# Attention outputs brought to one layout by sixteen transfers a batch and divided there, in place of turns on TensorE, in a three-stage decoder layer on one Trainium2 core

## What is computed

```python
q = q.reshape(B, N, H, D).transpose(0, 2, 1, 3)          # H = 16 heads, D = 16 dims
scores = jnp.einsum('bhqd,bhkd->bhqk', q, k) / jnp.sqrt(jnp.asarray(D, q.dtype))
attn = jax.nn.softmax(scores, axis=-1)
out = jnp.einsum('bhqk,bhkd->bhqd', attn, v)
out = out.transpose(0, 2, 1, 3).reshape(B, N, C)
return out @ Wo.T + bo
```

## Time and profile before

| | us |
|---|---|
| median of three executions | 1017.08 |
| lowest and highest | 1014.64 and 1022.38 |
| the profiled execution | 1020.84 |
| its span, from the first to the last instruction | 1019.1 |

### The profile page before, as it was taken

How to read it: one execution, slowest core, us unless ns; L and a number is a source line. 1 busy time by engine, 2 the same in 40 slices (tenths; PEclk the granted TensorE clock), 3 DMA queues, 4 the chain that set the end, 5 groups by cost and what they waited for, 6 DMA issues and landing times. The chain is left out here.

```text
span 1019.1 us, 16854 instructions
## 1 busy us (share of the span) xinstructions
PE 863.1 (85%) x5964; PEld 663.5 (65%) x5964; DVE 597.7 (59%) x1441; ACT 405.0 (40%) x623; POOL 354.1 (35%) x290
## 2 busy tenths in 40 slices
PE   5998947789899888988989888887279999999993
PEld 4776725455666566655666556544279999999993
DVE  4889751545675777667676666643235555555542
ACT  4565611145444444445444454443043334233320
POOL 0333352222233434344342443223212442244422
PEclk9999967679998999999999998877579999999997
DMA  3117302444443445444344442400343222343100
GB/s 115 42 43 210 108 24 78 113 106 126 104 126 115 109 111 125 124 113 114 103 124 121 117 114 74 116 21 24 106 135 109 94 88 90 113 128 106 46 22 22
DMA packets 73432, 98.82 MB, mean 97 GB/s; under 512 B 10529, under 2 KB 60874, under 8 KB 73376
## 3 DMA queue, kind: packets, MB, share of 16 engines
q1 hardware_dynamic: 69920, 89.95, 32.0%
q0 software_dynamic: 3456, 8.13, 2.2%
HBM read 63.40 MB, written 35.73 MB: 97 GB/s over the span
## 5 line engine op out<-in xcount | busy, mean ns | idle before, releaser
L946 DVE TENSOR_REDUCE nmax<-ps_m 128x4 f32<-128x1024 f32 x128 | 156.6, 1224 | 174.6 <-PE ps_m L711 172.1
L903 ACT ACTIVATE pt<-ps_a 128x1024 f32<-128x1024 f32 x128 | 131.1, 1025 | 89.7 <-PE ps_a L721 88.3
L1216 ACT ACTIVATE hid<-ps_h 128x640 fp32r<-128x640 f32 x64 | 45.1, 705 | 151.3 <-PE ps_h L1156 151.3
L1156 PE MATMUL ps_h<-xt,w_hi 128*128 128x320 f32 x512 | 99.9, 318 | 1.0 <-DVE xt L1231 1.0
L1168 PE MATMUL ps_y<-w_hi,hid 128*128 128x256 f32 x640 | 85.3, 284 | 1.7 <-issue 1.7
L1265 DVE SCALAR_TENSOR_TENSOR hid<-ps_h,hid 128x640 fp32r<-128x640 f32 x64 | 52.7, 824 | 56.2 <-ACT hid L1216 55.7
L1156 PEld LDWEIGHTS ps_h<-xt,w_hi 128*128 128x128 f32 x512 | 80.0, 191 | 5.5 <-DVE hid L1265 3.9
L1168 PEld LDWEIGHTS ps_y<-w_hi,hid 128*128 128x128 f32 x640 | 80.1, 192 | 1.9 <-issue 1.9
L721 PE MATMUL ps_a<-qst,kst 49*128 49x256 f32 x512 | 67.8, 345 | 15.5 <-ACT pt L903 15.2
L721 PEld LDWEIGHTS ps_a<-qst,kst 49*128 49x128 f32 x512 | 40.8, 197 | 57.0 <-issue 31.8
L711 PE MATMUL ps_m<-kst,qst 48*128 48x256 f32 x512 | 66.9, 342 | 11.1 <-DVE nmax L946 5.9
(11 more groups left out here) (169 smaller groups left out, 1654.9 us busy)
## 6 DMA issues: line engine op xcount, KB each, us to landing
halves_dram<-half SPq DMA_DIRECT2D x64, 256.0 KB, 2.4
gated<-in_w SPq DMA_DIRECT2D x16, 1024.0 KB, 5.4
kst<-halves_dram SPq DMA_DIRECT2D x64, 128.0 KB, 3.1
qst<-halves_dram SPq DMA_DIRECT2D x64, 128.0 KB, 3.2
rows_dram<-blank SPq DMA_DIRECT2D x1, 5160.0 KB, 19.7
gated<-rows_dram SPq DMA_DIRECT2D x8, 645.0 KB, 4.2
x_raw<-in_x_t SPq DMA_DIRECT2D x8, 512.0 KB, 3.9
xres<-in_x SPq DMA_DIRECT2D x16, 256.0 KB, 3.6
```

The source lines that it names most:

```text
L903: nc.scalar.activation(pt[:, k % 4].rearrange("p s t q -> p (s t q)"), ps_a[:].rearrange("p s t q -> p (s t q)"), ACT.Exp).then_inc(s["exp ...
L946: nc.vector.tensor_reduce(nmax[:, q, :, :, h // 2].rearrange("p t s -> p s t"), ps_m[:], AX.X, ALU.max, negate=True).then_inc(s["max_done" ...
L1156: mm = pe.matmul(ps_h[:, f % 2, c2, 0:HC], w1[a][:, p, k, f * P:(f + 1) * P], xt[:, b, p, k, c2 * HC:(c2 + 1) * HC], start=(n == 0 and k = ...
L1216: nc.scalar.activation(hid[:, HI, f, :].rearrange("p (c n) -> p c n", c=2), ps_h[:, f % 2, :, 0:HC], ACT.Relu).then_inc(s["hid_hi"], 1)
```

## The change

The turns and the division by query are taken out: `sums_by_query`, lines 1028 and 1029, the turn back and the ScalarE copy. Instead `oraw` is sent on by transfers within SBUF (`part`): for each half of the heads eight, each 16 partitions of 512 elements (32 KB), which bring the dims of all heads to `odim` and their sums to `osum`, both with channels on partitions. VectorE then takes the reciprocal of the whole `osum` (128x512) and multiplies, in slot 9 of step `j+3`. `project_out` moves from slots 12 and 13 to 11 and 12, the residual and statistics from slot 14 to 13, their mean from 15 to 14. On SP `part` for the second half of the heads stands between the stores of keys and of queries, and for the first half behind the load of the context; both waits for landed stores now stand behind the stores of the queries. In `vals` two heads share one block of ones (48 columns for a pair instead of 64), so that in the second half of the heads the sums stand ahead of the dims; the ScalarE copy into `vals` writes the same elements in another order. The rows of `w_o` and `bv` are reordered on the host to fit.

```diff
-    vals = T("vals", [P, 2, KT, NH, VW], F32)
+    vals = T("vals", [P, 2, KT, NP, VP], F32)
...
-    rec = T("rec", [P, NH], F32)
-    onrm = T("onrm", [P, KT, D], F32)
+    odim = T("odim", [P, KD, S], F32)
+    osum = T("osum", [P, KD, S], F32)
...
+    o_in = [[s["lo_in0"], s["lo_in1"]], [s["hi_in0"], s["hi_in1"]]]
+    OIN = 2 * PV * 16
...
-                sp.wait_ge(stored, j * 32 + 32)
+
+            def part(j, p, side):
+
+                settled(sp)
+                sp.wait_ge(s["oraw_hi" if side else "oraw_lo"], j + 1)
+                need(sp, s["ont_out"], j)
+                for i in range(PV):
+                    rows = slice(NP * HD // 2 * side + HD * i, NP * HD // 2 * side + HD * (i + 1))
+                    for tile, odd in ((odim, side), (osum, 1 - side)):
+                        first = VW * i + HD * odd
+                        sp.dma_start(tile[rows, :, :], oraw[first:first + HD, 2 * side:2 * side + 2, :]
+                                     ).then_inc(o_in[side][p], 16)
...
                     store(n, p, 0, s["k_split"], s["k_stored"])
+                if on(n, 3):
+                    part(n - 3, 1 - p, 1)
+                if on(n, 0):
                     store(n, p, 1, s["q_split"], s["q_stored"])
+                    settled(sp)
+                    sp.wait_ge(s["k_stored"], n * 32 + 32)
+                    sp.wait_ge(s["q_stored"], n * 32 + 32)
                     stack(n, p, 0)
                 if on(n, 0) and on(n, -1):
                     load_ctx(n + 1, 1 - p)
+                if on(n, 2):
+                    part(n - 2, p, 0)
...
-                        mm = pe.matmul(ps_o[VW * i:VW * (i + 1), g, :], vals[:, p, t, h, :],
+                        odd = g // 2
+                        mm = pe.matmul(ps_o[VW * i:VW * (i + 1), g, :],
+                                       vals[:, p, t, g % 2 * PV + i, HD * odd:HD * odd + VW],
...
-                    if h in (7, 9) and on(n, 3):
-                        sums_by_query(n - 3, (h - 7) // 2)
-                    if h == 11 and on(n, 3):
-                        pe.wait_ge(s["on_done"], 2 * (n - 3) + 2)
-                        turn(ps_e, onrm, s["ont_mm"])
-                    if h in (12, 13) and on(n, 3):
-                        project_out(n - 3, h - 12)
+                    if h in (11, 12) and on(n, 3):
+                        project_out(n - 3, h - 11)
...
-                    if h == 12 and on(n, 3):
-                        act.wait_ge(s["ont_mm"], n - 2)
-                        nc.scalar.copy(ont[:].rearrange("p k t -> p (k t)"), ps_e[:]).then_inc(s["ont_out"], 1)
...
-                    if h in (8, 10) and on(n, 3):
-                        t = (h - 8) // 2
-                        dve.wait_ge(s["ot_mm"], 2 * j + t + 1)
...
-                        oc.done(nc.vector.reciprocal(rec[:], o4[:, :, HD]))
-                        nc.vector.tensor_tensor(onrm[:, t].rearrange("p (h d) -> p h d", d=HD), o4[:, :, 0:HD],
-                                                rec[:, :, None].to_broadcast([P, NH, HD]), ALU.mult
-                                                ).then_inc(s["on_done"], 1)
-                    if h == 14 and on(n, 3):
+                    if h == 9 and on(n, 3):
+                        dve.wait_ge(o_in[0][q], use(j, OIN, q))
+                        dve.wait_ge(o_in[1][q], use(j, OIN, q))
+                        need(dve, s["oproj_mm"], j)
+                        oc.done(nc.vector.reciprocal(osum[:], osum[:]))
+                        nc.vector.tensor_tensor(ont[:], odim[:], osum[:], ALU.mult).then_inc(s["ont_out"], 1)
+                    if h == 13 and on(n, 3):
                         dve.wait_ge(s["oproj_mm"], j + 1)
```

More of the change, by code:

```diff
@@ L391, in attend @@
     VW = 2 * HD
+    VP = 3 * HD
     AL, WL = 3, 5
@@ L739, in weigh @@
                 mm.then_inc(s["pv_mm"], 1)
-            def sums_by_query(j, t):
-                if t == 0:
-                    pe.wait_ge(s["oraw_hi"], j + 1)
-                    need(pe, s["place_done"], j)
-                else:
-                    pe.wait_ge(s["on_done"], 2 * j + 1)
-                for g in range(4):
-                    mm = pe.transpose(ps_e[:, g * P:(g + 1) * P], oraw[:, g, t * P:(t + 1) * P], eye[:])
-                mm.then_inc(s["ot_mm"], 1)
             def project_out(j, t):
@@ L753, in project_out @@
                     pe.wait_ge(s["ont_out"], j + 1)
+                    need(pe, s["place_done"], j)
                 for k in range(KD):
@@ L841, in split_hi, with sums_out @@
                 nc.scalar.copy(half[:, 0], kq[:]).then_inc(hi, 1)
-            def sums_out(j, half_of, done):
+            def sums_out(j, p, half_of, done):
                 act.wait_ge(s["pv_mm"], NG4 * j + NG4 // 2 * (half_of + 1))
-                need(act, s["ot_mm"], 2 * j)
+                if not isinstance(j, int) or j > 0:
+                    act.wait_ge(o_in[half_of][1 - p], use(j - 1, OIN, 1 - p))
                 two = slice(2 * half_of, 2 * half_of + 2)
@@ L940, in step @@
                 dc = Steps(dve, s["d_step"], 1, n)
-                oc = Steps(dve, s["o_step"], 3, j)
+                oc = Steps(dve, s["o_step"], 2, j)
                 rc = Steps(dve, s["r_step"], 4, i)
@@ L1038, in step @@
                         stats(st2, c["r2"], s["stats2"])
-                    if h == 15 and on(n, 3):
+                    if h == 14 and on(n, 3):
                         mean_var(oc, st2, mv2, s["stats2"], j)
@@ L1408, in by_dim, with by_side @@
         return np.moveaxis(v.reshape(v.shape[:-1] + (KD, P // HD // 2, 2, HD)), -3, -1).swapaxes(-2, -3).reshape(v.shape)
+    def by_side(v):
+        return v.reshape((2, KD, D // 4) + v.shape[1:]).swapaxes(0, 1).reshape(v.shape)
     mix, att, ffn = "L0_attn_", "L0_xattn_", "L0_ffn_"
@@ L1423, in laid_out @@
     }
-    for n in "vo":
-        arrays["w_" + n] = a(att + "W" + n).T
+    arrays["w_v"] = a(att + "Wv").T
+    arrays["w_o"] = by_side(a(att + "Wo").T)
     for n in "qk":
```

16 lines of the change are left out of this document (7 added, 9 removed).

## The result

| | before | after |
|---|---|---|
| median, us | 1017.21 (four executions, 1014.64 to 1022.38) | 1094.32 (four, 1093.73 to 1098.82) |
| ratio, with 95% interval | 1 | 1.0761 (1.0710 to 1.0812) |
| span of the profiled execution, us | 1019.1 | 1092.4 |
| mean granted clock | 0.909 | 0.865 |

The changed kernel is 7.6% slower, 77 us. The prediction said slower, but by 13 us, and its range ended at 1047.

What follows compares the result with a forecast made beforehand. TensorE, 90% busy and answered by VectorE, was taken as the bound. Steps +5.7, end of the stage +2 and clock +5 made +13 us on the median of 1017.08: 1030 us, range 1004 to 1047 (about 8 in 10).

Steps and rivals of the forecast that it cites:

- the two places: TensorE waits for `ont` at the projection (+0.45 us) and for `y` at line 674 (+0.4 us) in a full-clock step.
- The turns at full clock: Removing three groups of four turns on TensorE saves 0.7, 1.2 and 1.0 us, 2.9 us a step at most.
- The wait for `y`: TensorE waits about 1.5 us ahead of line 674, since residual and statistics stand ahead of `y` on VectorE.
- The end: Last step, from `oraw` copy to residual: +4.1 us; the two steps before give back 2 us, net +2 us.
- I let four steps of the 13 get an added half-clock stretch, each at 1.2 us: TensorE's longer waits bring extra time at half clock in four of 13 steps: +5 us in all.
- the multiplication has a row: 0.68 us: VectorE's added 128x512 multiplication takes 0.68 us, read from the earlier trace.
- the wait of 2 us: TensorE reaches the projection's first half at 381.0 us and waits 2 us for `ont`, there at 383.0.
- The short operations end near 378.45: In the full-clock step VectorE's short operations end at 378.45 us, before the transfers land at 379.0 and release the reciprocal.
- The second place: Line 674, needing `y`, starts 5.25 us behind line 711 where it was 4.85: +0.4 us a step.
- a period of 31 to 33 us: Sign in the changed profile: time between two executions of the once-a-step line, counterpart of line 951.
- all four cases: Rivals: reciprocal 0.7 us (993 us, 15%), 1.9 us (1006, 15%), 4.4 us (1045, 12%); late transfers (1045, 13%).
- the short-reciprocal case (993): Rival: VectorE's reciprocal takes 0.7 us, so `ont` is ready before TensorE: -1.8 us a step, 993 us; chance 15%.

Runs made afterwards that it cites:

- e4_no_divide: The changed kernel with the reciprocal and the multiplication left out, so the result lacks the division: 1029.67 us, ratio 1.0116.
- e9_no_divide_stats_late: The changed kernel without reciprocal and multiplication, and with the residual and its statistics back behind `y`: 992.07 us, ratio 0.9758.
- e12_residual_late: The changed kernel with POOL's two tensor additions for the residual issued behind its small powers: 1076.95 us, ratio 1.0528.
- late-projection kernels: The changed kernel with projection in slots 13 and 14, statistics in 15; division whole, in halves or in quarters: 1095.54, 1045.48, 1053.69 us.

## Why the prediction was wrong, by its steps

**Right.** The bound and the two places: TensorE waits for `ont` and for `y`, and the reciprocal takes 3.35 us where 3.3 was worked out from the earlier trace rows. The Trainium skill, "VectorE: DVE Perf Modes", section "Walkthrough: the 8-slice pipeline in each mode", read as 8 cycles for each element, would have given 4.4; the trace disagrees with that reading. The turns at full clock: "2.9 us a step at most", and 2.9 were measured (30.96 to 28.07). The wait for `y`: about 1.5 us, and 1.57 were measured; the 5.25 us from line 711 to line 674 were 5.24 in `e4_no_divide`. The end: from the end of the `oraw` copy to the start of the residual the last step needs 14.5 us where the earlier trace rows have 9.5, +5.0 against +4.1. On the queues there was luck: the issue was too low (0.42 us against 0.59), the landing too high (3.0 against 2.0), and the two errors nearly cancelled.

**The step that failed: "I let four steps of the 13 get an added half-clock stretch, each at 1.2 us".** That is 5 us, 0.4 us a step. By the table half clock adds 4.37 us to the products of a full step after the change and 1.19 before it: 3.2 us a step. In the step shown, clock 0.50 follows the wait for `ont` and again the one for `y`, and even in `e9_no_divide_stats_late`, with neither wait, nine of the ten steps have a clock below 1.00. No row stood behind the number four. The earlier trace rows had shown what a long piece of idle time brings: a slice with 0.29 of 1.5 us of work, and clock 0.50 behind it. By the table it is also most of what the turns fell short by (25 us, where 2.9 us in 13 steps are 38), and part of why the order at the second place cost 36 us, where the prediction's own wait of 1.45 us in 13 steps makes 19.

**The term "the multiplication has a row: 0.68 us", and with it the wait of 2 us.** The row was of an operation with POOL's large operations elsewhere. Here POOL's additions run beside it, it takes 1.68 us in the median, and the wait is 3.1 us in the middle of the stage, 3.3 in the step shown. `e12_residual_late` shows both the cause and the price, 17 to 24 us: with the multiplication at 0.69 us the wait is 2.1 us, so the 2 us would have been right.

**A slip in the sum.** "The short operations end near 378.45" is line 1021's end, 380.35, less 1.9 us, the first two groups of turns together. The second group stands behind line 1021, so only the first group (0.7) and the two operations that go (0.65) may be taken off: 379.0. The other three steps in four then have no 0.55 us in hand, and the sum is +0.85 us in every step, 11 us instead of 5.7.

**The second place, "+0.4".** This is a net figure: the wait for `y` against a half of the projection (1.03 us) that moved ahead of line 711. Read alone it makes the reordering look cheap. Held against the kernel that has the gain in it (3.6 us from line 732 to line 695 in `e9_no_divide_stats_late`) it is 1.6 us a step, before any half clock, and it could have been left out of the change.

The sum of the misses, by the full step: forecast was +0.8 us (0.44 and 0.38 for the clock), measured +5.25. Of the 4.4 us between them 2.8 are half clock, 1.0 the multiplication and 0.4 the slip. In 13 steps 4.4 us make 58 of the 64 us between 1030 and 1094; the rest was not taken apart. The prediction's own sign, a period of 31 to 33 us, is missed in the same way: 37.3 in full steps. The rivals' list was short where it mattered: all four cases varied the duration of the reciprocal or of the transfers, none the price of a wait. And the short-reciprocal case (993) would not have come true with a short reciprocal either: with none at all the kernel needs 1029.

**What stays open.** The price of one reciprocal against four pieces in its place was measured on the kernel before (55 and 30 us); how it divides between waiting and clock, there and in the table, was read from traces, not isolated by a run. Why a wait is followed by half clock in one step and not in the next (line 695 in `e4_no_divide`) was not found. The idle ScalarE of the late-projection kernels was seen in the waits, but no run took it away.

## What to carry to other kernels

Ask first what is queued behind a new long instruction, not who needs its result: 3.35 us of VectorE ahead of a maximum cost 4.1 us for each batch in the changed kernel, and 3.4 in the old one, where nobody waits for its value. Price each part of a change against the kernel that has the gain in it, and count the half clock behind each wait: one wait of 2.4 us a step cost nearly twice what one of 1.3 and one of 1.0 did, though TensorE stood idle nearly as long. Where two edits come in one change, here the removal of turns and a reordering of one slot, time them apart: the first was worth -25 us, the second +36.

## What the runs showed of the hardware

- The reciprocal on VectorE, f32 in SBUF: 0.33 us for 128x32, 0.95 for 128x128, 1.75 for 128x256, 3.35 for 128x512. From the last two, 6.3 ns an element; a multiplication of 128x512 takes 0.69 us, and the estimate from the earlier trace rows has 1.04 ns an element for it.
- That multiplication, with both operands in SBUF, takes 0.69 us alone (all 16 in `e12_residual_late`) and 1.68 us in the median, 2.05 at most, in the changed kernel, where POOL works on SBUF tensors of 128x512 beside it. POOL's second addition took 1.60 us in the step shown, and 1.27 in the median of the kernel before.
- Transfers within SBUF of 16 partitions with 2 KB each take SP 0.59 us to issue and land after 2.0 us.
- In the step shown a wait of TensorE of 3.3 us is followed by a granted clock of 0.50, and so is one of 1.6 us behind it; products at that level take nearly twice as long (2.07 us where 1.03; 3.67 where 1.99). It does not follow each time: in `e4_no_divide` the same wait of 1.57 us has line 695 at 3.67 us behind it in one step and at 1.99 in the next.
